# Transposing the attention outputs by DMA, and a new order at the seam to the out projection

## The reference

```python
def xattn(x, context):                    # x 8x128x512, context 8x2048x384
    q, k, v = x @ Wq, context @ Wk, context @ Wv          # 8 heads of 64
    out = softmax(q @ k.T * 64**-0.5) @ v                 # by head
    return out @ Wo + bo                                  # "the out projection"
def attn(y):                              # one head of 512
    queries, keys, values = y @ Wq + bq, y @ Wk + bk, y @ Wv + bv
    probs = softmax(where(causal, -inf, queries @ keys.T), axis=1) / sqrt(512)
    return y + probs @ values
x = x + xattn(layernorm(x), ctx_768)
x = x + attn(layernorm(x))
x = x + ffn(layernorm(x))                 # relu(x @ w1.T + b1), float_quantize, @ w2.T
```

## Time and profile before

| | |
|---|---|
| median of 3 runs | 994.87 us (993.1 to 995.66) |
| the profiled execution | 993.46 us; its span 991.6 us |
| busy in the span | PE 952.3 us (96%), PEld 582.3 (59%), DVE 570.1 (57%), ACT 588.8 (59%), POOL 440.7 (44%) |
| DMA transposes of probabilities | 2 x 128, median 3.1 us from issue to landing |

### The profile page before, as it was taken

How to read it: one execution, slowest core, us unless ns; L and a number is a source line. 1 busy time by engine, 2 the same in 40 slices (tenths; PEclk the granted TensorE clock), 3 DMA queues, 4 the chain that set the end, 5 groups by cost and what they waited for, 6 DMA issues and landing times.

```text
span 991.6 us, 19444 instructions
## 1 busy us (share of the span) xinstructions
PE 952.3 (96%) x7472; PEld 582.3 (59%) x7472; DVE 570.1 (57%) x1024; ACT 588.8 (59%) x1103; POOL 440.7 (44%) x291
## 2 busy tenths in 40 slices
PE   3789999999999999999999999999997899999998
PEld 2356666666666666666666666666664445544443
DVE  6435655556565555555555656567775835565533
ACT  3357777777777777777777777777674131222220
POOL 3155556655555566555556655554545540000000
PEclk9899999999999999999999999999998999999999
DMA  8147666666766667666666657668768101013311
GB/s 286 64 99 153 132 128 128 131 126 139 154 132 129 129 128 129 130 152 134 129 130 130 130 125 144 122 127 162 150 118 175 39 1 43 1 43 96 96 32 75
DMA packets 295786, 115.85 MB, mean 117 GB/s; under 512 B 272528, under 2 KB 272528, under 8 KB 295696
## 3 DMA queue, kind: packets, MB, share of 16 engines
q1 hardware_dynamic: 281264, 86.82, 44.2%
q10 hardware_dynamic: 14432, 27.79, 9.5%
HBM read 45.36 MB, written 2.10 MB: 48 GB/s over the span
## 4 chain that ended last, share of the span: by engine, by line
PE 89%; DVE 4%; POOL 2%; DMA 1%; ACT 1%; issue 1%; ACTq 0%; SPq 0%; POOLq 0%; DVEq 0%
PE v_ps L362 27%; PE k_ps L362 25%; PE e_ps L362 14%; PE e_ps L403 9%; PE o_ps L423 6%; PE o_ps L426 3%; PE o_ps L593 3%; DMA wq_raw<-in_xwq 1%; PE v_ps L566 1%; DVE stats L1028 0%; DVE x_in L886 0%; ACTq L839 0%; DMA raw<-in_ctx_t 0%; PE k_ps L514 0%; POOL rstd L1191 0%
## 5 line engine op out<-in xcount | busy, mean ns | idle before, releaser
L1209 POOL TENSOR_TENSOR p_l<-p_f,p_h 128x1024 f16<-128x1024 f32 x128 | 278.3, 2174 | 311.5 <-ACT p_f L738 307.1
L927 DVE TENSOR_TENSOR k_l<-k_ps,k_h 128x512 f16<-128x512 f32 x128 | 88.5, 691 | 155.7 <-ACT k_h L710 155.7
L738 ACT ACTIVATE p_f<-e_ps,bias 128x512 f32<-128x512 f32 x256 | 176.5, 689 | 0.0
L736 ACT ACTIVATE p_h<-e_ps,bias 128x512 f16<-128x512 f32 x256 | 174.4, 681 | 0.1
L932 DVE TENSOR_REDUCE q_max<-e_ps 128x2 f32<-128x1024 f32 x128 | 156.5, 1223 | 14.4
L919 DVE TENSOR_TENSOR v<-v_ps,v 128x512 f16<-128x512 f32 x128 | 88.8, 694 | 112.7 <-ACT v L702 112.5
L362 PE MATMUL v_ps<-wv_h,ctx_h 128*128 128x256 f16 x768 | 127.5, 275 | 4.7 <-DVE v L919 3.2
L362 PE MATMUL v_ps<-wv_h,ctx_l 128*128 128x256 f16 x768 | 126.4, 274 | 0.0
L362 PE MATMUL v_ps<-wv_l,ctx_h 128*128 128x256 f16 x768 | 126.3, 274 | 0.0
L1201 POOL TENSOR_TENSOR ctx_l<-raw,ctx_h 128x1536 f16<-128x1536 f32 x32 | 99.0, 3095 | 28.3 <-ACT ctx_h L691 28.3
L702 ACT ACTIVATE v<-v_ps 128x512 f16<-128x512 f32 x128 | 76.2, 595 | 51.8 <-PE v_ps L362 51.5
(11 more groups left out here) (151 smaller groups left out, 1248.4 us busy)
## 6 DMA issues: line engine op xcount, KB each, us to landing
raw<-in_ctx_t ACTq DMA_DIRECT2D x26, 768.0 KB, 5.0
w_raw<-in_w_t SPq DMA_DIRECT2D x32, 256.0 KB, 2.7
raw<-in_ctx_t SPq DMA_DIRECT2D x6, 768.0 KB, 4.7
pt_h<-p_h SPq DMA_TRANSPOSE x128, 3.1
pt_l<-p_l SPq DMA_TRANSPOSE x128, 3.1
xr<-in_x ACTq DMA_DIRECT2D x8, 256.0 KB, 4.9
out<-xr SPq DMA_DIRECT2D x8, 256.0 KB, 2.0
x_in<-in_x SPq DMA_DIRECT2D x4, 256.0 KB, 5.2
```

What stands on the lines that cost most here:

```text
L736: act.activation(p_h[:, s % H_RING, h, :], e_ps[s % 2][:, h, :], ACT.Exp, scale=EXP_SCALE, bias=bias[:, n % 2, h, q:q + 1]).then_inc(p_hi, 1)
L738: act.activation(p_f[:, s % F_RING, h, :], e_ps[s % 2][:, h, :], ACT.Exp, scale=EXP_SCALE, bias=bias[:, n % 2, h, q:q + 1]).then_inc(p_ful ...
L927: dve.tensor_tensor(k_l[:, n % 2, cols], k_ps[:, :], k_h[:, n % 2, cols], ALU.subtract).then_inc(k_split, 1)
L1209: pool.tensor_tensor(p_l[:, s % L_RING, :, :], p_f[:, s % F_RING, :, :], p_h[:, s % H_RING, :, :], ALU.subtract).then_inc(p_split, 1)
```

## The change

1. **The output of a batch leaves POOL in halves.** `o_norm` writes its product to a small fp32 tile `o_f`, casts that into a high half and subtracts for the low half: four POOL operations for two. The halves of a batch are in `o_half`, in the place of `o_all`.
2. **SP transposes them by DMA** (`turn_output`): two transposes of 128x512 a batch, into the columns of that batch's queries in `q_h` and `q_l`. SP waits for the batch's last stage, inside the loop after the `p_l` of slot 16b+19, and for the last batch after the loop. `turn(0, r)`, its evictions on ACT and DVE, and the tiles `ot_h` and `ot_l` as such are gone.
3. **The out projections** use `v_ps`, `k_ps` and the four banks of `e_ps`; they follow the weighted values of slots 123 to 127, and batch 7's stands behind the turns of rows 0 to 3 for the self attention.
4. **The x loads** are spread: rows 6 and 7 after slot 124 on ACT, rows 0, 1, 2 after slots 125 to 127, rows 3, 4, 5 after the loop.
5. **POOL and DVE** have a new order in the seam (last hunks).

```diff
-    out_turned, ot_end = place(nc, ctx1_base, [("ot_h", [P, DCH, B * T], F16), ("ot_l", [P, DCH, B * T], F16)])
+    ot_h, ot_l = q_h, q_l
-        turns = [(0, r) for r in range(B - 1)] + [(1, 0), (1, 1), (0, B - 1)] + [(1, r) for r in range(2, B)] + \
-            [(2, r) for r in range(B)]
+        turns = [(1, r) for r in range(B)] + [(2, r) for r in range(B)]
         def out_bank(r):
-            return t_bank[r % 2 if r < 4 else r - 4]
+            return [v_ps, k_ps, t_bank[0], t_bank[1], v_ps, k_ps, t_bank[2], t_bank[3]][r][:, :]
 # SP
+            def turn_output(b):
+                sp.wait_ge(o_ready, PAIRS * b + PAIRS)
+                for i, half in enumerate((ot_h, ot_l)):
+                    sp.dma_start_transpose(half[:, :, b * T:b * T + T], o_half[:, b, i, :]).then_inc(ot_landed[b], 16)
...
+                if s >= 19 and s % 16 == 3:
+                    turn_output((s - 19) // 16)
+            turn_output(B - 1)
 # PE
             def turn(what, r):
+                pe.wait_ge(xn2_ready, at + 1)
+                if at < 2:
+                    pe.wait_ge(x1_ready, 5 + at)
...
             def project_out(r):
-                pe.wait_ge(tr_split, turn_at(0, r) + 1)
+                pe.wait_ge(ot_landed[r], 32)
                 if r == 0:
                     pe.wait_ge(wx_split, 4)
+                    pe.wait_ge(v_split, SLOTS)
+                elif r == 1:
+                    pe.wait_ge(k_split, SLOTS)
+                elif r in (2, 3):
                     pe.wait_ge(p_full, 2 * SLOTS - 2)
+                elif r in (4, 5):
+                    pe.wait_ge(x1_ready, r - 3)
+                else:
                     pe.wait_ge(p_full, 2 * SLOTS)
...
-            for s in range(SLOTS, SLOTS + DRAIN):
+            for s in range(SLOTS, SLOTS + PV_LAG):
                 steady(s)
-                for r in {0: (0, 1), 1: (2,), 2: (3,), 3: (4,), 4: (5,), 5: (6,)}.get(s - SLOTS, ()):
-                    turn(0, r)
-                if s > SLOTS:
-                    project_out(s - SLOTS - 1)
+                for r in ((0, 1), (2,), (3,), (4,), (5, 6))[s - SLOTS]:
+                    project_out(r)
             turn(1, 0)
             turn(1, 1)
-            project_out(6)
-            turn(0, B - 1)
             turn(1, 2)
             turn(1, 3)
             project_out(7)
 # ACT, in the loop
+                if s == SLOTS - 4:
+                    for r in (6, 7):
+                        load_x(r, 0)
+                if s >= SLOTS - 3:
+                    load_x(s - SLOTS + 3, s - SLOTS + 16)
 # ACT, after the loop
-            act.wait_ge(wx_split, 16)
-            for r in range(B):
-                act.dma_start(xr[:, r, :], x[r]).then_inc(xr_landed[r], 16)
+            for r in (3, 4, 5):
+                load_x(r, 16)
 # DVE
+            steady(SLOTS)
+            for s in range(SLOTS + 1, SLOTS + PV_LAG + 1):
                 steady(s)
-                    turned_low(0, r)
+                residual(s - SLOTS - 1)
                 if s > SLOTS + 1:
                     norm(s - SLOTS - 2)
+            residual(5)
+            norm(4)
             turned_low(1, 0)
             turned_low(1, 1)
             residual(6)
             norm(5)
-            turned_low(0, 7)
             turned_low(1, 2)
             norm(6)
             turned_low(1, 3)
 # POOL, o_norm(n)
+                pool.tensor_tensor(o_f[:, :, :], o_sum[:, :, :], o_rec[:, :, :].broadcast_to([P, 2, DH]), ALU.mult)\
+                    .then_inc(o_f_ready, 1)
+                pool.wait_ge(o_f_ready, n + 1)
+                hi, lo = [o_half[:, b, i, p * P:p * P + P].rearrange("p (h d) -> p h d", h=2) for i in range(2)]
+                pool.tensor_copy(hi, o_f[:, :, :]).then_inc(o_hi, 1)
+                pool.wait_ge(o_hi, n + 1)
+                pool.tensor_tensor(lo, o_f[:, :, :], hi, ALU.subtract).then_inc(o_ready, 1)
 # POOL, after the loop
+            add_bias(0)
+            p_low(SLOTS - 2)
+            add_bias(1)
+            p_low(SLOTS - 1)
+            o_norm(STAGES - 2)
+            add_bias(2)
+            inverse_deviation(0)
+            for r in range(3, 6):
+                add_bias(r)
+                inverse_deviation(r - 2)
+            o_norm(STAGES - 1)
+            for r in (6, 7):
+                add_bias(r)
+                inverse_deviation(r - 2)
+            for r in (6, 7):
+                inverse_deviation(r)
```

More of the change, by code:

```diff
@@ L38 @@
 F_RING, H_RING, L_RING, T_RING = 2, 3, 2, 3
-DRAIN = 7
 EARLY_CTX = 6
@@ L122, in perceiver_kernel @@
     (o_all, ident, causal, bo_row, bv_row, b2_row, bq_col, bk_col, b1_col, b2_half, stats, mean_var, rstd, exponent,
-     q_max, bias, low, fade, acc, o_rec, o_sum) = keep.values()
+     q_max, bias, low, fade, acc, o_rec, o_sum, o_f) = keep.values()
     q_h, q_l = queries.values()
@@ L135, in perceiver_kernel @@
     w_dram = [xwo, awq, awk, awv]
-    ot_h, ot_l = out_turned.values()
+    ot_h, ot_l = q_h, q_l
+    o_half = waiting["o_half"]
     at_h, at_l = turned.values()
@@ L209, in perceiver_kernel @@
         o_sum_ready = sem("o_sum_ready")
+        o_f_ready = sem("o_f_ready")
+        o_hi = sem("o_hi")
+        ot_landed = [sem(f"ot_landed{b}") for b in range(B)]
         o_ready = sem("o_ready")
@@ L537, in project @@
                 if i < 4:
-                    pe.wait_ge(x1_ready, 5 + i)
+                    pe.wait_ge(x1_ready, (3, 4, 7, 8)[i])
                 else:
@@ L774, in load_weight, with load_x @@
                     .then_inc(wx_landed[k], 16)
+            def load_x(r, after):
+                if after:
+                    act.wait_ge(wx_split, after)
+                act.dma_start(xr[:, r, :], x[r]).then_inc(xr_landed[r], 16)
             def steady(s):
@@ L805, in _ @@
                     load_weight(s - SLOTS + 20)
+                if s == SLOTS - 4:
[3 more added lines that the diff above has]
+                    load_x(s - SLOTS + 3, s - SLOTS + 16)
             def turned_high(what, r):
                 act.wait_ge(tr_filled, turn_at(what, r) + 1)
-                dst = ot_h if what == 0 else at_h
-                act.activation(dst[:, :, r * P:r * P + P], turn_bank(what, r)[:, :].rearrange("p (c n) -> p c n", c=DCH),
+                act.activation(at_h[:, :, r * P:r * P + P], turn_bank(what, r)[:, :].rearrange("p (c n) -> p c n", c=DCH),
                                ACT.Copy).then_inc(tr_hi, 1)
@@ L835, in hidden_round @@
                                scale=1.0 / W1_SCALE, saturate=False).then_inc(h_q8, 1)
-            act.wait_ge(wx_split, 16)
-            for r in range(B):
-                act.dma_start(xr[:, r, :], x[r]).then_inc(xr_landed[r], 16)
-            for s in range(SLOTS, SLOTS + 6):
+            for r in (3, 4, 5):
+                load_x(r, 16)
+            for s in range(SLOTS, SLOTS + X_LAG):
                 steady(s)
-                for r in {0: (0, 1), 1: (2,), 2: (3,), 3: (4,), 4: (5,), 5: (6,)}.get(s - SLOTS, ()):
-                    turned_high(0, r)
-            for turned_at in range(B - 1, B + 5):
-                turned_high(*turns[turned_at])
+            for r in range(5):
+                turned_high(1, r)
             act.wait_ge(small_landed, 96)
@@ L1020, in turned_low @@
                 rows = slice(r * P, r * P + P)
-                hi, lo = (ot_h, ot_l) if what == 0 else (at_h, at_l)
-                dve.tensor_tensor(lo[:, :, rows], turn_bank(what, r)[:, :].rearrange("p (c n) -> p c n", c=DCH),
-                                  hi[:, :, rows], ALU.subtract).then_inc(tr_split, 1)
+                dve.tensor_tensor(at_l[:, :, rows], turn_bank(what, r)[:, :].rearrange("p (c n) -> p c n", c=DCH),
+                                  at_h[:, :, rows], ALU.subtract).then_inc(tr_split, 1)
             def row_moments(i):
```

36 lines of the change are left out of this document (3 added, 33 removed).

## The result

The changed kernel takes 983.02 us (median of 6 runs, 981.86 to 984.81), the kernel before 994.23 beside it: a ratio of 0.9892, 95% interval 0.9879 to 0.9906. The profiled execution took 983.69 us, its span 981.9, 9.7 less than before. Forecast were 983.8 and, for a profiled execution, 982.4.

What follows compares the result with a forecast made beforehand. PE bounds the kernel, with time to win only in the seam at 750 to 794.2 us; its steps put the query projection at 783.2 against 794.2, 11.0 less than 994.87: 983.8 us on the median, range 979.5 to 988.5.

Steps and rivals of the forecast that it cites:

- The cause of the stall: In the seam, ACT issues eight x loads (4.82 us) before slot 126's biases, so PE waits 6.26 us at 758.75.
- The sum: Seam steps on ACT, PE, POOL and DVE added up: query projection starts at 783.2 against 794.2, 11.0 us less.
- bias of slot 126: On ACT in the seam: comes at 751.5 instead of 754.73, with three loads still ahead of it.
- last output: POOL's final attention output in the seam, made by 773.2.
- The stage-30 output: On POOL in the seam: four operations where it was two, 4 x 0.49 = 1.9 us, done at 761.6.
- The clock: After PE's idling at 772 to 778, batch 7's out projection runs slow: charged 4.2 us instead of 2.6.
- The transposes: Last batch's 128x512 DMA transposes: landing taken as 3.1 us, bounds 1.5 and 10.8, landed at 777.5.
- norms would take 1.5 us beside POOL's additions: On DVE in the seam: a norm takes 1.48 us beside POOL's bias addition, 0.52 without it.
- The steady part: Loop: p_h some 2 us late once in 16 slots, hidden by 8.7 us of cover; cost 0, bounds -0.5 and +5.
- Late transposes: Rival, chance 0.15: last two transposes land after 778.5 and PE waits; at worst landing gain 4.4, time 990.5.
- The seam nearer its floor: Rival, chance 0.09: DVE's norms not slowed by POOL and clock stays up; gain 14.4, 980.5; floor 977.2.
- SP held: Rival 'Slower', chance 0.04: in the steady part output transposes delay p_l; about 1074 us at worst landing.

Runs made afterwards that it cites:

- b_loads: Kernel before with only the x loads spread as in the change: 990.06 us, ratio 0.9969 to before, seam 40.60 us for 43.87.
- a_loads_late: Changed kernel with all eight x loads issued after the loop again: 988.30 us, ratio 0.9949 to before, seam 37.17 us.
- a_norm_alone: Changed kernel with POOL's roots and bias additions reordered so the norms of rows 0 and 4 don't run beside an addition: 980.81 us, ratio 0.9872 to before.
- a_last_x2: Changed kernel with the last batch's pair of transposes made twice, PE waiting for the second pair: 984.41 us, ratio 0.9908 to before.
- a_warm: Changed kernel with 18 extra unused matmuls of 512 columns in PE's idle stretch of the seam: 981.33 us, ratio 0.9879 to before.
- best2: Changed kernel with POOL's biases and roots, DVE's accumulations and rests, and x loads rearranged in the seam, PE's order kept: 977.13 us, ratio 0.9840 to before.
- a_hold_x3: Changed kernel with the transpose pairs of batches 0 to 6 made three times, PE waiting for the last: 1008.10 us, ratio 1.0145 to before.
- a_hold_x5: Changed kernel with the transpose pairs of batches 0 to 6 made five times, PE waiting for the last: 1067.14 us, ratio 1.0740 to before.

## Why the prediction was right

**The cause of the stall.** Read from the chain of waits: eight DMA issues on ACT in front of the exponentials. b_loads shows that moving them is worth 3.27 us. It does not show that their time on ACT is the only cost: a_loads_late has the second one, the late landing of slot 125's `p_l`, which the prediction did not see. Before, PE came to that transpose (763.46) after it had landed (762.65), so the 6.26 us there are ACT's.

**The sum.** From the start of the seam the prediction has the out projection of batch 7 at 28.15 us (778.5) and the kernel has it at 28.41; the query projection at 32.85 for 33.57. The steps between were met within 0.7 us: bias of slot 126 at 751.5 for 751.95; PE without a real wait to 771.7, for 771.97; last output at 773.2 for 773.0; the turns of rows 2 and 3 ending at 778.5 for 779.2. The stage-30 output took 1.74 us (760.10 to 761.84) for 1.9, its cast 0.29 where 0.49 was taken.

**What was mis-sized.** The clock: it fell before the turns of rows 2 and 3, so these took some 0.87 each instead of 0.44, and the projection of batch 7 took 4.72 where I had taken 4.2 from a row in which part of it already ran fast again. Together 1.3 us too little, of which 0.7 is left at the end of the sum, since other steps came a little earlier. The gain between the two profiled executions, 9.7 against 11.0, lacks this 0.7 and the 0.6 outside the seam. That the medians (994.23 to 983.02, a gain of 11.2) come closer to 11.0 than the mechanism does is luck: the profiled execution before was faster than its median, and the one after slower.

**The transposes.** Bounded at 1.5 and 10.8 and taken at 3.1; the sixteen of 128x512 landed in 2.4 to 4.0, median 2.5, of which the issue is 1.19. The upper bound, the 10.8 of the earlier trace rows, was no property of the transpose: it is the one issued at 751.85 beside the eight x loads, and the change takes its cause away. The rule of the Trainium skill that spoke against the change (page "VectorE: DVE Perf Modes", section "The three transpose paths", 1309 ns for a block by DMA) does not hold here as a price by the block: four blocks landed in 2.5 us, eight in 3.1. Its preference for TensorE is not tested alone. A DMA transpose is slower than a turn of 0.44 us, but it stands on a queue that had time, and the turn brings an eviction on ACT and one on DVE with it; with the new order around it that was worth 6.70 us of the seam.

**POOL and DVE.** That norms would take 1.5 us beside POOL's additions was read from two rows of before; a_norm_alone shows it is their company. The Trainium skill, page "GPSIMD Engine Reference", section "Specifications", says that GpSimd's SBUF interfaces are shared with VectorE, with contention for VectorE instructions in a 2-port perf mode or with two SBUF inputs. The runs agree as far as they go: the norms take 0.55 us alone and 1.47 to 1.48 beside, while residuals and moments, which have one SBUF input tensor, are not held. In which mode the norm works no run shows.

**The steady part.** Costed at nothing behind a cover of 8.7 us; PE is as full as before, p_h goes out late by the expected 2 us (177.38, where before it stood 2.7 us behind the p_l, at 175.5), and the cover measures 8.2 to 8.5. POOL's busy time grew by 21.64 us in 30 stages (60 operations more), 0.7 a stage where 1.0 was put.

**The rivals.** Late transposes: refuted by a_last_x2. The seam nearer its floor: the mechanism is real (a_norm_alone, a_warm), but it needs another order than the change has; best2 is that case. SP held: real as well, but past a delay of some 8.4 us only, and the change makes the `p_l` 0.9 us late.

## What to carry to other kernels

At a seam where each engine's order is written by hand, add up the critical engine's own work first (26.1 us here): what is longer than that is handoffs, and they can be followed row by row to a fraction of a microsecond. Work that nobody waits for yet (bias additions, loads) belongs in the idle time of the loop before, not in the queue that everyone waits for; DMA issues are such work too, on the engine that issues them, and the bytes behind them can keep another queue's transfer from landing (10.3 us for 3.9). And when a gap on TensorE is priced, the slower matmuls behind it belong in the price, turns included.

## What the runs showed that I had not expected

- Half the size saves little of a DMA transpose: 128x512 lands in 2.5 us for 3.1 and is issued in 1.19 for 1.23. Beside a context load the second of a pair landed only after 5.6 us (181.89 to 187.47).
- The profile put PE's waits for landed transposes in a_hold_x3 and a_hold_x5 down to "issue" (194.83, 202.67): only SP's timeline told what was late.
- Eight x loads issued in a row made a transpose of another queue land 10.3 us after its issue (752.00 in a_loads_late), where 3.1 is the median.
- Beside a bias addition on POOL, DVE's norm ended only some 0.28 us after the addition, while its residuals and moments took no longer than alone.
- A delay of the landing by 3.7 us came out as 0.64 at the end of the seam, less than at its middle (1.07), since the clock was back sooner (the projection took 4.30 us, 780.56 to 784.86, for 4.72).
